# A two-layer mixture-of-experts block: result additions placed later, the slot table split in two halves of products, the epilogue and the first expert tiles reordered, and the second biases kept in SBUF

## The reference, cut to what matters

```
x = x + attention_a(layernorm(x))      # 16 heads, latent 32
x = x + experts(layernorm(x))          # layer 1
x = x + attention_b(layernorm(x))      # 16 heads of 8
x = x + experts(layernorm(x))          # layer 2

def experts(h):                        # E = 8 experts, F = 512
    topv, topi = top_k(h @ gate_w + gate_b, 2)
    we = softmax(topv)                 # weights of the two chosen experts
    return sum over the two: we * (gelu(h @ W1[e] + b1[e]) @ W2[e] + b2[e])
```

## Time and profile before

| | |
|---|---|
| median of 3 runs | 1199.89 us (1197.47 to 1200.57) |
| the profiled execution | 1191.1 us, of which the span is 1189.4 us |
| PE busy, PEld busy | 1024.3 us (86%), 793.5 us (67%) |
| DVE, ACT, POOL busy | 747.3 us (63%), 648.2 us (55%), 758.7 us (64%) |
| mean granted TensorE clock | 0.908 of full speed |

### The profile page before, as it was taken

How to read it: one execution, slowest core, us unless ns; L and a number is a source line. 1 busy time by engine, 2 the same in 40 slices (tenths; PEclk the granted TensorE clock), 3 DMA queues, 4 the chain that set the end, 5 groups by cost and what they waited for, 6 DMA issues and landing times. The chain is left out here.

```text
span 1189.4 us, 29763 instructions
## 1 busy us (share of the span) xinstructions
PE 1024.3 (86%) x11227; PEld 793.5 (67%) x11227; DVE 747.3 (63%) x1845; ACT 648.2 (55%) x1193; POOL 758.7 (64%) x824
## 2 busy tenths in 40 slices
PE   4799999999988987999877899999988878999820
PEld 3566776676765666999874556666655557999820
DVE  5878888888889954622345677777777626322332
ACT  1476777776755543455445667767755424455410
POOL 2788988888876746277663477667534233577765
PEclk9799999999998897999997999999988658999975
DMA  9100011010000023578940000000000024688732
GB/s 263 4 2 20 19 38 37 20 37 16 6 11 2 11 72 93 162 232 251 217 121 1 1 15 24 25 16 23 13 8 4 10 98 133 182 239 222 241 104 68
DMA packets 69805, 91.10 MB, mean 77 GB/s; under 512 B 15074, under 2 KB 49762, under 8 KB 69666
## 3 DMA queue, kind: packets, MB, share of 16 engines
q1 hardware_dynamic: 58226, 68.98, 18.4%
q0 software_dynamic: 9088, 18.63, 7.3%
q10 hardware_dynamic: 2352, 1.58, 0.5%
HBM read 68.45 MB, written 20.71 MB: 75 GB/s over the span
## 5 line engine op out<-in xcount | busy, mean ns | idle before, releaser
L1417 ACT ACTIVATE PT<-PS 128x768 f32<-128x768 f32 x256 | 207.1, 809 | 133.0 <-PE PS L1925 79.2
L608 POOL TENSOR_SCALAR_AFFINE_SELECT PT<-PT 128x512 f32<-128x512 f32 x256 | 179.4, 701 | 144.1 <-ACT PT L1417 143.5
L621 POOL DMA_INDIRECT xg<-normed,source x156 | 148.0, 949 | 94.8 <-DVE source L1101 48.1
L1448 ACT ACTIVATE hid<-PS,b_cols 128x256 f32<-128x256 f32 x312 | 122.5, 475 | 113.3 <-PE PS L1664 110.5
L1983 PE MATMUL PS<-W,hid 128*128 x1248 | 158.9, 283 | 0.1
L1983 PEld LDWEIGHTS PS<-W,hid 128*128 128x128 f32 x1248 | 152.6, 199 | 0.6 <-issue 0.5
L730 POOL DMA_INDIRECT got<-expert_rows,slot_of x128 | 122.7, 959 | 40.2 <-issue 34.4
L1311 DVE TENSOR_TENSOR y_rows<-PS,b_rows 128x256 f32<-128x256 f32 x78 | 33.1, 425 | 149.0 <-PE PS L1983 144.1
L1755 PE MATMUL PS<-PT,v_aug 128*32 128x256 f32 (+1 forms) x2048 | 117.9, 352 | 2.2 <-POOL PT L608 2.1
L1737 PE MATMUL PS<-causal_b,ident_b 128*128 128x256 bf16 x512 | 104.1, 287 | 13.5 <-DVE q_aug L1260 12.9
L1662 PE MATMUL PS<-xg_hi,w_ring 128*128 128x256 f32 x312 | 96.9, 311 | 16.7 <-DVE xg_lo L1167 13.0
(11 more groups left out here) (301 smaller groups left out, 2993.2 us busy)
## 6 DMA issues: line engine op xcount, KB each, us to landing
w_ring<-halves_w SPq DMA_DIRECT2D x78, 512.0 KB
expert_rows<-y_rows SPq DMA_DIRECT2D x78, 128.0 KB, 3.1
normed<-xn SPq DMA_DIRECT2D x16, 256.0 KB, 2.3
xg<-normed,source POOLq DMA_INDIRECT x156
W<-in_L_ffn_w_dram SPq DMA_DIRECT2D x1, 2048.0 KB, 13.8
halves_w<-w_hi SPq DMA_DIRECT2D x8, 256.0 KB, 2.3
halves_w<-W SPq DMA_DIRECT2D x8, 256.0 KB, 2.0
got<-expert_rows,slot_of POOLq DMA_INDIRECT x128, 2.7
```

Source lines behind the costliest of these rows:

```text
L608: nc.gpsimd.affine_select(out=diagonals, in_=diagonals, pattern=[[0, 4], [1, P]], compare_op=ALU.is_ge, fill=0.0, base=0, channel_multipli ...
L621: nc.gpsimd.indirect_dma_start(out=xg[:, i % AHEAD, b_, :], out_offset=None, in_=normed if i >= EARLY else normed[0:NH * P, :], in_offset= ...
L1417: s.activation(PT[:, unit % 2, pair, :, :, :], PS[:, 4:6, 0:3 * P].rearrange("p h (a q) -> p a h q", q=P), ACT.Exp).then_inc(m["exp_done"], 1)
L1448: ins = s.activation(hid[:, r % 2, k, :], h_bank[r % 2][k // 2][:, k % 2 * ROWS:(k % 2 + 1) * ROWS], ACT.Gelu, bias=b1_cols[:, bass.ds(e * ...
```

## The change

- The second biases `b2_rows` get their own place in SBUF and are loaded once, with the other weights. DVE's wait at the end of the epilogue and the two loads after the epilogues go.
- `LAST` runs `out_t` and `out` ahead of the `gate` of chunk 6. The first tile is turned after `out_t`, the second after that `gate`, followed by `up(0)`; `up(1)` moves from the epilogue into the expert loop. ACT normalizes the last chunk ahead of the gelu of tile 0. DVE splits tile 2 within the last `choose`.
- In iteration 0 PE runs `up(1)`, `down(0)`, `up(2)` and only then `ranks`.
- `TABLE_AT` is 6, and `tokens_of` runs its first 16 products before `down(6)` and its last 16 after it. The second half's table covers only the 60 blocks of tiles 9 to 38, not all 78.
- `ADDED_AT` is 32. Tiles 32 to 38 add 21 results. The other 11 are added in layer 1 during the first four units of attention b and in layer 2 after the loop. The two statistics move from tiles 31 and 34 to 34 and 37.

```diff
-ADDED_AT = FIRST_DONE + 5
+ADDED_AT = FIRST_DONE + 9
-TABLE_AT = 5
+TABLE_AT = 6
@@ PlanA (Plan gets the same new order)
-    LAST = [("turn", 1, 0, 7), ("gate_t", 0, -1, 0), ("gate", 0, -1, 1), ("out_t", 0, 0, 2), ("out", 0, 0, 3), ...
+    LAST = [("turn", 1, 0, 7), ("gate_t", 0, -1, 0), ("out_t", 0, 0, 2), ("out", 0, 0, 3), ("gate", 0, -1, 1), ...
@@ SP
+            sp.dma_start(b2_rows[...], b2...partition_broadcast(P)).then_inc(bias_loaded, 16)
-                sp.wait_ge(attended[n], 1)
-                sp.dma_start(b2_rows[...], b2...partition_broadcast(P)).then_inc(me["bias_ready"], 16)
@@ DVE, close
+                            if part == 0:
+                                split_rows(me, 2)
@@ DVE, attention b, chunk 0
+                        if adds_at(unit):
+                            add_results("1", adds_at(unit))
@@ DVE, experts
-                dve.wait_ge(m["bias_ready"], 16)
+                dve.wait_ge(bias_loaded, 16)
-                    if i + 2 < TILES:
+                    if 0 < i < TILES - 2:
                         split_rows(m, i + 2)
-                    if n == "1" and i == ADDED_AT + 3:
+                    if n == "1" and i == ADDED_AT + 2:
-                    if n == "1" and i == ADDED_AT + 6:
+                    if n == "1" and i == ADDED_AT + 5:
@@ ACT, last_chunk
+                normal(n, st.c, gate_norm_b(st.c), st.c, range(CT), 1 if n == "b" else 0)
                 act.wait_ge(b1_loaded, 16)
                 gelu(me, 0)
-                normal(n, st.c, gate_norm_b(st.c), st.c, range(CT), 1 if n == "b" else 0)
@@ PE, experts
+                    if i == 0:
+                        up(m, 1)
+                        down(0)
+                        up(m, 2)
+                        pe.wait_ge(m["mask_ready"], 2)
+                        ranks(1, y_bank[1]).then_inc(m["rank_ready"], 1)
+                        continue
-                    if 0 < i < TILES - 1:
+                    if 1 < i < TILES - 1:
                         up(m, i + 1)
                     if i == TABLE_AT:
                         pe.wait_ge(m["hots_ready"], 2)
                         pe.wait_ge(m["y_ready"], i)
-                        tokens_of(1, y_bank[(i + 1) % 2][:, 0:BLOCKS]).then_inc(m["table_ready"], 1)
+                        tokens_of(1, table, 0)
                     down(i)
-                    if i == 0:
-                        pe.wait_ge(m["mask_ready"], 2)
-                        ranks(1, y_bank[1]).then_inc(m["rank_ready"], 1)
+                    if i == TABLE_AT:
+                        pe.wait_ge(m["hots_ready"], 3)
+                        tokens_of(1, table, 1).then_inc(m["table_ready"], 1)
```

More of the change, by code:

```diff
@@ L163 @@
     FIRST_CLOSE = [None, None, ("prep", 0, 1), None, ("value", 0, 1), None, ("prep", 0, 2), ("turn", 0, 0)]
-    LAST = [("turn", 1, 0, 7), ("gate_t", 0, -1, 0), ("gate", 0, -1, 1), ("out_t", 0, 0, 2), ("out", 0, 0, 3), ("gate_t", 0, 0, 4), ("gate", 0, 0, 5)]
+    LAST = [("turn", 1, 0, 7), ("gate_t", 0, -1, 0), ("out_t", 0, 0, 2), ("out", 0, 0, 3), ("gate", 0, -1, 1), ("gate_t", 0, 0, 4), ("gate", 0, 0, 5)]
     def __init__(self):
@@ L218 @@
     FIRST_LATE = [("key", 2, 0), ("key", 3, 0), ("prep", 0, 1), ("key", 0, 1), ("key", 1, 1), ("key", 2, 1), ("key", 3, 1), ("prep", 0, 2)]
-    LAST = [("turn", 1, 0, 7), ("gate_t", 0, -1, 0), ("out_t", 0, 0, 1), ("gate", 0, -1, 2), ("out", 0, 0, 3), ("gate_t", 0, 0, 4), ("gate", 0, 0, 5)]
+    LAST = [("turn", 1, 0, 7), ("gate_t", 0, -1, 0), ("out_t", 0, 0, 2), ("out", 0, 0, 3), ("gate", 0, -1, 1), ("gate_t", 0, 0, 4), ("gate", 0, 0, 5)]
     BY_ACT = ("key", "out_t", "gate_t")
@@ L297, in adds_in @@
     k = ADDS * (i - ADDED_AT)
-    end = RESULTS if i == TILES - 1 else min(k + ADDS, RESULTS)
-    return range(k, end) if i >= ADDED_AT else range(0)
+    return range(k, k + ADDS) if i >= ADDED_AT else range(0)
+ADDED = ADDS * (TILES - ADDED_AT)
 def split_at(unit):
@@ L1093, in sources @@
             def sources(me, at):
[L1095 to L1096 removed]
+                late = slice(EARLY * RB, BLOCKS)
+                own.did(v.tensor_scalar(table2[:, 0, late], at, 0.0, float(NH * P), ALU.is_gt, ALU.mult))
+                own.then(v.tensor_copy(table2[:, 1, late], at))
                 v.memset(mark[:, 2:3], 0.0).then_inc(me["table_copied"], 1)
[L1098 to L1101, removed]
+                own.then(v.tensor_tensor(table2[:, 0, late], table2[:, 0, late], table2[:, 1, late], ALU.add))
+                own.then(v.tensor_tensor(table2[:, 0, EARLY * RB:FIRST_BLOCKS], table2[:, 0, EARLY * RB:FIRST_BLOCKS],
+                                         table1[:, EARLY * RB:], ALU.add))
+                own.then(v.tensor_scalar(table2[:, 1, late], table2[:, 0, late], -1.0, 0.0, ALU.add, ALU.max))
+                v.tensor_copy(source[:, late], table2[:, 1, late]).then_inc(me["slots_ready"], 1)
             def early_experts():
@@ L1184, in close @@
                         statistics(m, NCH - 1, 1 if n == "b" else 0)
+                    if s.kind == "gate" and s.c == NCH - 2:
+                        dve.wait_ge(m["freed_dve"], s.freed)
+                        split_rows(me, 0)
                         split_rows(me, 1)
@@ L1385, in _ @@
             experts("2")
+            add_results("2", range(ADDED, RESULTS))
             for c in range(RESULTS // (2 * CT), NCH):
@@ L1681, in ranks, with tokens_of @@
                 return ins
-            def tokens_of(h, at):
-                for k in range(2):
-                    for t in range(NH):
-                        ins = t_.matmul(at, lane_hot[:, k, :, t], block_hot[:, k, 0:BLOCKS if h else FIRST_BLOCKS, t], start=(k + t == 0),
-                                        stop=(k == 1 and t == NH - 1), skip_group_check=True)
+            def tokens_of(h, at, k, tiles=range(NH)):
+                blocks = slice(EARLY * RB, BLOCKS) if h else slice(0, FIRST_BLOCKS)
+                for t in tiles:
+                    ins = t_.matmul(at, lane_hot[:, k, :, t], block_hot[:, k, blocks, t], start=(k + t == 0),
+                                    stop=(k == 1 and t == NH - 1), skip_group_check=True)
                 return ins
@@ L1783, in first_tiles @@
             def first_tiles(m, s):
-                if (s.kind, s.c) == ("gate_t", NCH - 2):
+                if s.kind == "out_t":
                     pe.wait_ge(m["slots_ready"], 1)
                     turn_rows(m, 0)
-                elif s.kind == "out_t":
+                elif (s.kind, s.c) == ("gate", NCH - 2):
                     turn_rows(m, 1)
-                elif s.kind == "out":
                     pe.wait_ge(experts_loaded, 32)
                     up(m, 0)
-                    up(m, 1)
             def attention_a():
```

45 lines of the change are left out of this document (24 added, 21 removed).

## The result

The changed kernel takes 1210.7 us (median of 5 runs) against 1199.89 us: ratio 1.0129, 95% interval [1.0095, 1.0164]. A second set of runs of it, `after_again`, gives 1.0121 [1.0074, 1.0168]. Ratios and intervals here compare runs in the fast state alone. The quotient of the two medians is only 1.0090: the five runs of the kernel before reach from 1186.8 to 1204.8 us, so sizes are taken from the ratios. The direction is as forecast and 1210.7 lies in the range, but the forecast was +0.6% and the mean of the two ratios is +1.25%, some 15 us and not 7.3: more than twice the size.

The account below looks back on a forecast made before the run. PE was taken to bound the expert layers, and POOL, when late, the join to attention b. Terms -1.0 - 2.5 + 11.8 - 4.0 + 1.0 + 2.0 = +7.3 us, put on the median, gave 1207.2 us; range 1197 to 1214.

Parts of the forecast that it names:

- The results: Later result additions and statistics in both layers and attention b: -4.0 + 1.0 + 2.0 us.
- Layer 2, -4.0: Results of layer 2: later additions remove PE's 3.24 us stop and 1.7 of slow clock, less some late weights: -4.0.
- The join, +1.0: Layer 1 into attention b: POOL's later root and gathers use up the 8.20 us cover: +1.0 (bounds 0 and +4).
- root-to-keys sum: POOL at the join: two roots and 16 gathers, 2.6 + 20.2 us, from 605.6 to the keys at 628.4.
- Attention b, +2.0: Three additions, 1.06 us, in each of four units, on DVE's loop: 4 x 0.5 = +2.0 (bounds 0 and +4).
- Rival 2: Result gathers are the bottleneck; ordinary runs wait longer for results, which the delay covers: -5.0, 1194.9 us; chance 0.14.
- rival 3: Late weights stop PE in layer 2 too; POOL queue and additions cost their upper bounds: 1214.8 us; chance 0.10.
- Rival 1: Transitions keep full clock through the first tiles, giving 3.0 and 5.4 instead of 1.0 and 2.5: 1202.3 us; chance 0.17.
- The table: Turn of tile 9: PE waits 6.9 us for gathers after the late products; +5.9 per layer, +11.8 for two.
- the 6 to 7.5 that the forecast named as its sign: In each layer PE turns tile 9 after an idle of 6 to 7.5 us released by the gather.
- The transitions: Attention into the expert layers: bias wait gone, new order; -1.0 in layer 1, -2.5 in layer 2.
- The 1.5 us of slow clock: Start of an expert layer: half clock on up(3) after PE's idle of about 3 us behind the rank copy: about 1.5.

Follow-up runs that it names:

- b_adds_l2: The kernel before with the later additions in layer 2 only; ratio 0.9986 [0.9954, 1.0018], -1.7 us.
- b_adds_l1: The kernel before with the later additions and statistics in layer 1 and attention b only; ratio 1.0051 [1.0017, 1.0084], +6.1 us.
- b_late_table: The kernel before with only the late, split table of 60 columns; ratio 1.0099 [1.0067, 1.0131], +11.9 us.
- a_ranks_first: a_order_bias with the rank products moved ahead of down(0) and up(2) in iteration 0; ratio 0.996 [0.9929, 0.999].
- a_filler: The changed kernel with 28 unused constant products of 512 columns behind the table's last product; ratio 1.0046 [1.0011, 1.0082].
- a_order_bias: The changed kernel with table and additions put back, keeping resident biases, new order and 60-column table; ratio 0.9963 [0.9926, 1.0].
- b_bias_only: The kernel before with only the resident biases, DVE's wait for the bias load gone; ratio 0.993 [0.9896, 0.9964].

## Why the forecast was too small

Term by term, the forecast against what was measured:

| | forecast | measured |
|---|---|---|
| bias and order, with the 60 columns | -3.5 - 1.6 = -5.1 | -4.4 |
| late table, on that base | +11.8 + 1.6 = +13.4 | +14.5, alone +11.9 |
| additions, layer 2 | -4.0 | -1.7 |
| additions, join and attention b | +1.0 + 2.0 | +6.1 |
| sum | +7.3 | +14.5 by these rows, +15.0 by the ratio |

(The 1.6 is twice the 4.82 - 4.0 by which the forecast's table term already had the narrower products. The two rows of additions are from `b_adds_l2` and `b_adds_l1`.)

**The step that failed is the term "The results".** It stood at -1.0, and alone on the kernel before the same edit costs +5.0 us, interval 1.6 to 8.6, which the forecast lies outside. Against the 7.7 us that are missing that is some 6. On the base of the changed kernel the sign isn't settled (+4.9 or -3.2, by the chain), so the share of each term there stays open.

- *Layer 2, -4.0.* The step read one stop of 3.24 us with 1.7 of slow clock behind it and took it for what every execution pays. The mechanism is right: with the later additions no wait for a result over 0.5 us is left in DVE's queue there, in any of nine profiles. The size is not: the first addition waits 3.42 us in the profile of before and 2.58, 2.14, 2.06, 1.81, 1.41 and 1.14 in six other kernels with the same place for it; in the seventh, `b_late_table`, the longest wait is the second addition's, 0.77. The mean gain is 1.2 by the traces and 1.7 by the ratio.
- *The join, +1.0.* The root-to-keys sum held: 614.42 to the keys at 637.35 is 22.9 us, forecast 22.8. f31 to the first keys is 1.2 us longer over the profiles. f27 to f31 adds 0.8 and the way to the first `q_aug` 0.6, for which no step had a term; both are within what single profiles scatter.
- *Attention b, +2.0.* Half of 4 x 1.06 was taken for covered. The units 0 to 7 take 3.4 us longer, so only a fifth is. One group took 1.50 us, not 1.06.

Rival 2, faster because ordinary runs wait longer for results, is refuted: moving these additions alone gives -1.7 us, not -8 or more. Of rival 3 the half on the join and the additions happened in part (it put +5 on top of the forecast's +3.0, and +3.1 on top was measured), its late weights did not: PE's longest idle at the results of layer 2 is 0.98 us in the changed kernel. So although its sum, +14.9, is what the ratio says, that is a coincidence. Rival 1, transitions at full clock, did not happen (`up(1)` at 0.41 to 0.56 us a product against 0.28 at full clock).

**The table was right in kind, and somewhat too small.** Forecast in the changed kernel: 5.4 of other work, 4.0 of products, a wait of 6.9, slow clock 1.5. Measured in layer 1: 1.8 for `down(5)`, 1.6 for turn and `up(7)`, 1.8 for `down(6)`, which is 5.2; products 1.9 and 2.1; a wait of 7.38; and from the turn of tile 9 to the next 5.4 us instead of 3.4, 2.0 of slow clock. That is +6.6, forecast +5.9. In layer 2 the wait is 8.40, outside the 6 to 7.5 that the forecast named as its sign, and the same count gives +7.6: 17.56 us from the start of `down(5)` (1028.95) to the turn, 11.68 in the kernel before (1014.12 to 1025.80), and 1.7 of slow clock behind it. Together they are +14.2 for +11.8. The Trainium skill (TensorE: Matmul & The Clock Gate, section HAM oscillation) says that a matmul loop with a DMA wait in it starts its next block at the low clock; the clock of 0.55 in the wait and the `down` of 2.52 behind it agree. Against the kernel with the same columns at tile 5 the stretch f0 to f7 grows by 8 us in each layer, against before by 6.5: the narrower products had a gain in them that the late table hides.

The 60-column product, interpolated at 0.124 us, took 3.96 / 32 = 0.124. An estimate from the Trainium skill (same page, section LDWEIGHTS), 32 weight loads of 128 columns, puts the 32 at 3.4 us whatever their columns; the traces disagree, 3.1 for 46 columns, 4.0 for 60 and 5.0 for 78. The kernel reads both operands of these products with a step of 16 values, and no run has them side by side, so whether the columns alone or their step sets the price is open.

**The transitions came out near in size, but not by the forecast's course.** The `finish` of tile 4 is 0.5 and 2.0 us earlier against attention's last output copy, forecast 1.0 and 2.5. But the forecast had the rank copy 3.0 earlier at full clock or 1.0 later at half, and chose nearer the first. It is level in layer 1 (24.8 us behind that copy, 25.0 before) and 1.2 earlier in layer 2, since `up(1)` and most of `down(0)` ran at half clock ahead of it. That the blocks ahead of the ranks are the cause is shown by `a_ranks_first`, that it is not worth much by its ratio: the table's chain from products to landed rows comes next. The 1.5 us of slow clock that the term had behind an idle of 3 didn't come either: PE idles 0.49 and 1.97 us around `down(1)`, and the `up(3)` behind runs at a clock of 1.00. Two faults of opposite sign, so the size is near by luck.

Open: the 7 us between the ratio of `a_filler` and its trace; what the additions cost on the base of the changed kernel; whether the 0.8 us at f27 to f31 is real; and what makes the first result of layer 2 late in one execution and not in another.

## What to carry to other kernels

A producer that feeds a chain over several engines (products, source rows, gathers) should be placed by the work left behind it, not by the work ahead of it: here 5.2 us of work (6.5 with a slow `down`) nearly cover a chain of 7 to 8, and moving it one tile later costs 12 us alone and 14 or more on the narrower table. A wait removed in front of such a chain can move into it, so look for the next wait before counting the gain. And the size of a stop seen in one profile is one draw: compare the same stop in the other layer and in profiles of sibling kernels before a term of the sum rests on it.

## What the runs showed of the hardware

- Filling a wait with work didn't hold the clock each time. In `a_filler` the granted clock was 1.00 through the 28 products and through the 2.03 us of idle behind them in layer 1, and 0.55 in the `up` after that; the `down` took 2.36 us. In layer 2, with 1.38 us of idle, it stayed at 1.00 and the `down` took 1.95.
- At the start of layer 1 of the changed kernel the granted clock was 0.50 for the 4.7 us that PE had worked without a gap ahead of `down(0)`, and 0.60 in `down(0)`, whose 16 products took 3.0 us; only in the `up` behind it was it 1.00. Ahead of those 4.7 us PE had waited 1.49 us.
- Two profiles can mislead by more than the effect looked for: `a_order_bias` has a span of 1183.4 us and `b_bias_only` one of 1196.9, and their medians are 1192.95 and 1191.68.
